# A three-layer graph kernel: 32 row slots in place of 16, indices listed 16 columns at a time, and one semaphore for the four gathers of a group

## What is computed

```
def _rgcn_conv(x, src, dst, edge_type, edge_weight, W, root, bias):
    xj = x[src]
    m = jnp.zeros((xj.shape[0], W.shape[2]), dtype=x.dtype)
    for r in range(W.shape[0]):
        mask = (edge_type == r).astype(x.dtype)[:, None]
        m = m + mask * (xj @ W[r])
    m = m * edge_weight[:, None]
    out = jax.ops.segment_sum(m, dst, num_segments=x.shape[0])
    return out + x @ root + bias
...
msgs = edge_weight[:, None] * x[row]
agg = jax.ops.segment_sum(msgs, col, num_segments=x.shape[0])
return agg @ W.T + b
...
h = jnp.maximum(_layernorm(x, axis=-1), 0.0)
x = x + _L0_gnn_ref(h, edge_index, edge_type_4, edge_weight, ...)
h = jnp.maximum(_layernorm(x, axis=-1), 0.0)
x = x + _L1_gnn_ref(h, edge_index, edge_weight, L1_gnn_W, L1_gnn_b)
```

## Time and profile before

| | |
|---|---|
| Median of 3 runs | 7402.78 us (7398.44 to 7409.87) |
| Span of the profiled execution | 7521.5 us |
| POOL busy | 4442.7 us (59% of the span) |
| PE busy | 3965.3 us (53%), PEld 3719.1 us (49%) |
| DVE busy | 2144.3 us (29%) |
| ACT busy | 502.6 us (7%) |
| Granted clock, mean over the span | 0.623 of full speed |
| DMA | 356.64 MB, 47 GB/s |

### The profile page before, as it was taken

The page is one execution under the profiler, slowest core; times in us unless marked ns, Lnnn a source line. Parts: engine busy times, 40 slices in busy tenths (PEclk is TensorE's granted clock), DMA queues, the critical chain, the costliest instruction groups (busy, mean ns, idle before and its releaser), DMA issues.

```text
span 7521.5 us, 80234 instructions
## 1 busy us (share of the span) xinstructions
PE 3965.3 (53%) x17451; PEld 3719.1 (49%) x17451; DVE 2144.3 (29%) x8672; ACT 502.6 (7%) x1663; POOL 4442.7 (59%) x4701
## 2 busy tenths in 40 slices
PE   3665666555555565665565556663434343343444
PEld 3555555555555555555555555553333333333333
DVE  3332233333332322333323323342222222222222
ACT  3000000000000100000000000021000000000000
POOL 3665666566665565665566556645656666666665
PEclk6666666666666666667677767665555555555555
DMA  4111111111111211111111111112111111111112
GB/s 112 45 45 44 45 45 45 44 45 44 45 44 44 72 45 44 44 45 43 44 44 45 44 44 45 45 52 54 44 42 43 42 43 43 43 43 43 42 43 70
DMA packets 250630, 356.64 MB, mean 47 GB/s; under 512 B 80254, under 2 KB 175586, under 8 KB 250610
## 3 DMA queue, kind: packets, MB, share of 16 engines
q0 software_dynamic: 150048, 307.60, 15.6%
q1 hardware_dynamic: 92262, 44.91, 2.1%
q10 hardware_dynamic: 8300, 3.92, 0.2%
HBM read 330.44 MB, written 25.67 MB: 47 GB/s over the span
## 4 chain that ended last, share of the span: by engine, by line
another core or an unknown queue 45%; PE 24%; issue 17%; DVE 6%; DVEq 6%; ACT 1%; ACTq 1%; DMA 0%; POOL 0%; SPq 0%; POOLq 0%
PE bank L547 13%; PE bank L527 10%; DVE window L756 3%; DVEq L735 3%; DVE acc L739 1%; DVEq L756 1%; DVE idx L748 1%; ACT agg L437 1%; DVEq L748 1%; ACT node L378 0%; PE bank L519 0%; PE bank L515 0%; DVEq L739 0%; PE bank L587 0%
## 5 line engine op out<-in xcount | busy, mean ns | idle before, releaser
L312 POOL DMA_INDIRECT rows<-table,idx x4689 | 4430.2, 945 | 3004.4 <-DVE idx L748 1506.2
L547 PE MATMUL bank<-window,rows 128*128 128x192 f32 (+1 forms) x9378 | 2595.9, 442 | 1138.0 <-DVE window L756 711.1
L547 PEld LDWEIGHTS bank<-window,rows 128*128 128x128 f32 x9378 | 2245.0, 292 | 1258.9 <-issue 655.2
L739 DVE TENSOR_TENSOR acc<-acc,bank 128x48 f32 x1173 | 240.1, 205 | 4920.9 <-remote 3406.8
L756 DVE TENSOR_SCALAR window<-iota,key_col,sw 128x192 f32<-128x192 f32 x3126 | 1001.4, 383 | 0.4 <-DVE key_col L693 0.2
L527 PEld LDWEIGHTS bank<-agg,W2s 128*128 128x128 f32 x3128 | 612.8, 281 | 744.7 <-issue 429.3
L527 PE MATMUL bank<-agg,W2s 128*128 128x48 f32 x3128 | 597.6, 354 | 699.5 <-ACT agg L437 433.7
L527 PEld LDWEIGHTS bank<-agg,W1s 128*128 128x128 f32 x3128 | 603.3, 278 | 701.0 <-ACT agg L437 416.4
L527 PE MATMUL bank<-agg,W1s 128*128 128x48 f32 x3128 | 591.6, 351 | 650.6 <-ACT agg L437 398.5
L527 PE MATMUL bank<-agg,W3T 128*128 128x48 f32 x782 | 248.4, 418 | 994.3 <-ACT agg L437 970.5
L437 ACT ACTIVATE agg<-bank 128x192 f32<-128x192 f32 (+1 forms) x1173 | 330.0, 289 | 6220.5 <-remote 4202.1
(11 more groups left out here) (66 smaller groups left out, 592.1 us busy)
## 6 DMA issues: line engine op xcount, KB each, us to landing
rows<-table,idx POOLq DMA_INDIRECT x4689
table<-node SPq DMA_DIRECT2D x48, 256.0 KB
table<-node SPq DMA_DIRECT2D x7, 896.0 KB
tile_rows<-table SPq DMA_DIRECT2D x98, 64.0 KB
tile_rows<-in_x_dram SPq DMA_DIRECT2D x97, 64.0 KB
out_dram<-node SPq DMA_DIRECT2D x24, 256.0 KB
node<-in_x_dram SPq DMA_DIRECT2D x6, 896.0 KB, 11.4
node<-in_x_dram SPq DMA_DIRECT2D x1, 832.0 KB
```

The costliest lines, as they stand in the source:

```text
L312: eng.indirect_dma_start(out=rows[:, slot, :], out_offset=None, in_=table[r][:, :], in_offset=bass.IndirectOffsetOnAxis(ap=idx[:, slot:slo ...
L547: ins = eng.matmul(agg_ps[q % 2][:, 0:width], rows[:, slot, :], window[:, q % 2, k, 0:width], start=(k == 0), stop=(k == n - 1))
L739: eng.tensor_tensor(a, a, mix_ps[q % 2][:, 0:W], ALU.add).then_inc(s_acc, 1)
```

## The change

The loop iteration becomes eight groups (`GI = 8`, two halves of `HALF = 4`), and so there are 32 row slots, and 49 iterations to a layer in place of 98. `idx`, `rows` and `sw` double. The staging tile for the ends of the layers, and the sum of the general path, which doesn't run on these inputs, lie now inside `rows`. DVE lists the indices and weights of four groups at once: at `q == 1` those of the second half of the same iteration, at `q == 5` those of the first half of the next. POOL waits for a list once in four groups. The four gathers of a group signal one semaphore, for which PE waits once, ahead of the group's first matmul. In the diff the first `fast(r)` is that of POOL; the piece with `s_agg_sb` is PE's, and those with `list_half` are DVE's.

```
-GI = 4
+GI = 8
 NSLOT = CG * GI
+HALF = GI // 2
...
+    OWN = GI // HALF
...
-        stage = sb("stage", [P, BS, TB * P])
...
+        stage = rows[:, 0:BS * TB, :].rearrange("p (s t) d -> p s (t d)", s=BS)
+        gagg = rows[:, BS * TB:BS * TB + R, :].rearrange("p t d -> p (t d)")
...
-        s_row = [sem(f"s_row{k}") for k in range(NSLOT)]
+        s_row = [sem(f"s_row{q}") for q in range(GI)]
...
             def fast(r):
                 def group(i, g, q, n):
-                    eng.wait_ge(s_idx, g + (r * NG + 1))
-                    hold(eng)
+                    if q % HALF == 0:
+
+                        eng.wait_ge(s_idx, i * OWN + (r * NT + q // HALF + 1))
+                        hold(eng)
                     for k in range(q * CG, q * CG + n):
-                        gather(r, k, s_row[k])
+                        gather(r, k, s_row[q])
...
                     if not first(g, 2):
                         eng.wait_ge(s_agg_sb, g + (r * NG - 1))
+                    eng.wait_ge(s_row[q], i * (16 * CG) + (row_base(r, q) + 16 * n))
                     for k in range(n):
                         slot = q * CG + k
-                        eng.wait_ge(s_row[slot], i * 16 + (row_base(r, slot) + 16))
                         ins = eng.matmul(agg_ps[q % 2][:, 0:width], rows[:, slot, :], window[:, q % 2, k, 0:width],
                                          start=(k == 0), stop=(k == n - 1))
...
+                def list_half(i, h):
+
+                    m = HALF * CG
+                    if isinstance(i, int):
+                        m = min(m, C - (i * NSLOT + h * m))
+                    k = h * HALF * CG
+                    c = i * NSLOT + k
+                    eng.tensor_copy(idx[:, k:k + m], src_col[:, bass.ds(c, m)]).then_inc(s_idx, 1)
                     if r < 2:
-                        scale_weights(q * CG, q * CG, CG)
+                        eng.tensor_scalar(sw[:, k:k + m], w_col[:, bass.ds(c, m)], extg[:, 3:4], wscale[:, 0:1],
+                                          ALU.add, ALU.mult).then_inc(s_sw, 1)
+                for h in range(OWN):
+                    list_half(0, h)
...
                         eng.wait_ge(s_agg, g + (T - 1))
-                        if not (isinstance(g, int) and g + 2 >= NG):
-                            m = min(CG, C - (g + 2) * CG) if isinstance(g, int) else CG
-                            k = ((q + 2) % GI) * CG
-                            eng.tensor_copy(idx[:, k:k + m], src_col[:, bass.ds(g * CG + 2 * CG, m)]).then_inc(s_idx, 1)
-                            if r < 2:
-                                scale_weights(g * CG + 2 * CG, k, m)
-                    if r < 2:
-                        eng.wait_ge(s_sw, g + (T + 1))
+                    if q == 1 and not first(i, 1):
+                        list_half(i, 1)
+                    if q == HALF + 1 and not (isinstance(i, int) and i == NI - 1):
+                        list_half(i + 1, 0)
+                    if q % HALF == 0 and r < 2:
+                        eng.wait_ge(s_sw, i * OWN + (r * NT + q // HALF + 1))
```

More of the change, by code:

```diff
@@ L59, in build @@
     split_last = last_rows < P
-    assert D == P and NI == NT and NG - (NI - 1) * GI >= 3 and NG <= 512
+    assert D == P and NI * OWN == NT and NG - (NI - 1) * GI >= HALF + 3 and NG <= 512 and NI > 2
     assert R * P <= 512 and 4 * CT * P + C <= ACC and NB > BS
@@ L110, in build @@
         gwindow = window[:, :, :, :].rearrange("p a c w -> p (a c w)")[:, 0:R * P]
-        gagg = stage[:, 0, :]
+        stage = rows[:, 0:BS * TB, :].rearrange("p (s t) d -> p s (t d)", s=BS)
+        gagg = rows[:, BS * TB:BS * TB + R, :].rearrange("p t d -> p (t d)")
         gtmp = sb("gtmp", [P, 8])
@@ L235, in build, with row_base @@
         stored_all = stored[2] + 16 * (NB - 1 + moves(last_batch))
-        def row_base(r, slot):
-            return 16 * r * (NI - 1 + (slot < last_chunks))
+        def row_base(r, q):
+            return 16 * r * ((NI - 1) * CG + min(CG, max(0, last_chunks - q * CG)))
         block = ctx.enter_context(nc.Block())
@@ L432, in group @@
                 def group(i, g, q, n):
-                    if q == 0 and r < 2:
-                        own(r, i)
+                    if q % HALF == 0 and r < 2:
+                        own(r, i * OWN + q // HALF)
                     eng.wait_ge(s_agg, g + (r * NG + 1))
@@ L551, in group @@
                         mix_group(g - 1, q - 1 + GI)
[L552 to L555, removed]
+                    if q % HALF == 0 and r == 0:
+                        own_turn(i * OWN + q // HALF)
+                    if q % HALF == 1 and r < 2:
+                        own_root(r, i * OWN + q // HALF)
                 over_groups(eng, group)
@@ L760, in group @@
                         add_window(g - 2, q)
-                    if q == 2:
+                    if q % HALF == 2:
                         eng.wait_ge(s_acc, g + (T - 1))
-                        own(r, i)
-                        eng.wait_ge(s_own, i + (r * NT + 1))
+                        own(r, i * OWN + q // HALF)
+                        eng.wait_ge(s_own, i * OWN + (r * NT + q // HALF + 1))
                 eng.wait_ge(s_zero, min(r + 1, 2))
```

6 lines of the change are left out of this document (removed).

## The result

The changed kernel takes **7753.94 us** (median of 4 runs, 7744.41 to 7761.5); the kernel before 7406.32 (4 runs, 7398.44 to 7415.0: the three of the table above, and a fourth of 7415.0). The ratio is **1.047, 95% interval 1.045 to 1.048**: slower, as forecast, and 176 us under the forecast 7930.

The account below looks back on a forecast made before the run. It took PE's results, held back while gathers stream, to set the pace. (782 x 6.9) + (391 x 6.2) + 240.9 = 8061 us of span, times 0.984 gave 7930 us, 7.1% slower; range 6850 to 8650.

Parts of the forecast that it names:

- The hold: PE's results wait while POOL's gathers stream and come out together 3.68 to 5.50 us after the last gather's start.
- Later copies: DVE lists after every fourth addition while POOL stands: 6.53 to 7.5 us a group in layers one and two, 7.0 halfway.
- The third layer's 6.2: Four additions already follow a release there, so the index copy can come right at it: 6.2 us a group.
- The factor 0.984: Runs' median over profiled span (7402.78 / 7521.5), used to turn 8061 us of span into 7930 us.
- Fewer copies: On DVE, 1161 index copies become 98 a layer; 0.1 us a group taken as saved, ends 0 and 0.29.
- one semaphore: PE can't start on a group's first chunk before its fourth lands; 11 us in all, 0.15%, at layer starts.
- longer loop: Half as many loop turns and fewer waits on POOL lie under the hold; shared staging costs nothing.
- The shared port: DVE's copies cost POOL's gathers next to nothing; by the skill, fewer copies would free some 170 us at most.
- Rival 1: The hold goes and POOL runs through at 1.25 us a gather: 6010 us; chance 0.10.
- Rival 2: Gather runs join into 32, as DVE lists while POOL still gathers: 5.77 us a group, 6900 us; chance 0.22.
- Rival 3: PE's own work makes its true ends late; pace stays 6.2 us a group, time near 7400; chance 0.06.

Follow-up runs that it names:

- e1_sem: The kernel before with only one edit: the four gathers of a group signal one semaphore, for which PE waits once; 6091.6 us, ratio 0.9992.
- e5_after: The changed kernel, unedited, measured again beside the kernel before on the second chip; 6088.98 us, ratio 0.999.
- e7_fine2: The changed kernel with lists of four columns at each group, two groups ahead, on the second chip; 6089.32 us, ratio 0.9988.
- e6_before: The kernel before, unedited, measured once more on the second chip; 6097.81 us.

## Why the prediction was right, and where it was off

**The hold**, "PE's results are held back while gathers stream, and come out together some us after the last one": right as a reading of that trace. The bursts, the runs and the gaps are there after the change, and 4.00 us pass from last gather to release where the earlier trace rows had 3.68 to 5.50 (that 5.50 ends at an ACT copy, the others at an addition). It was wrong to think that it belongs to any execution of this kernel: on two of the three chips used later it was absent, and there the change gains 0.1%. That the changed kernel met the hold when it was first measured was luck, for nothing in the prediction says when it comes; the sign of the forecast hung on it.

**Later copies**: the mechanism is right, and its best case is what happened. I worked out 26.1 us for the cycle of the first layer and took 7.0 us a group, half way to the worst pattern with two additions between release and list. That pattern did not come: four additions fell to a cycle, two of them under the gathers as in the earlier trace rows, and the cycle was 26.3 (26.0 and 26.2 on average in the first two layers). **The step that was mis-sized is this term**: 6.9 us a group on the books, 6.48 measured, 782 x 0.42 = 328 us too much. The third layer's 6.2 was 6.22, but only in part by its own reasons: single runs took 6.11 a group, and joined ones, which the term left out, 6.34.

**The factor 0.984** between profiled span and median went the other way. It was no relation of span and time: in every run on record the time lies some 2 us above the span of the same execution (7761.5 and 7759.7 for the profiled one here). The profiled execution of the kernel before was a slower one, with 7521.5 outside its timed runs of 7398.44 to 7415.0 and near the 7511 of the third chip. So 125 us that I took off should have stayed. Against the sum of 8061 us of span: -328 for the first term, +9 for the third layer, +18 outside the stretches gives 7760. With the factor the two errors cancel in part, which is luck: -301 + 125 = -176 us.

**Fewer copies**, **one semaphore** and **longer loop**: small, as said. Where no hold covers them e1_sem, e5_after and e7_fine2 each lie 4 to 8 us below the kernel before, 0.1%; for e1_sem the interval includes no difference. The 0.1 us a group taken for the fewer copies under the hold was tested by no run. The +18 us outside the stretches were not in the sum. None lies before the first gather, which starts at 94.9 us in both traces. Some 3 come from the earlier trace rows, whose stretches end about 1 us later than those here; the other 15 lie behind the last gather of each layer (42.1 us to the next layer's first for 36.8, 77.3 for 74.9, 44.7 to the end for 37.3). Without the hold, in e5_after and e6_before, the same three differ by 0.5, 1.9 and 1.3 us, and not in one direction. What makes them longer under the hold wasn't looked into.

**The shared port**: e7_fine2 and e5_after differ by 879 index copies and take 6089.32 and 6088.98 us. The loss that I worked out by the Trainium skill, SBUF - State Buffer, part on DVE blocking DMA, does not show here; a gather takes 946 ns in both.

**Rival 1**, the hold goes: its picture and its time came true (6010 stated, though 6102 x 0.984 is 6004; 6089 measured), for both kernels and for another reason than the change. **Rival 2**, runs join: it was right that they can, and 26 runs in the third layer did. Its price was wrong. The joined run shown takes 51.1 us from 6106.82 to 6157.87, 6.38 a group and not 5.77, because behind the release, 5 us after the last gather, three more additions had to pass before the list, where my price had none. So joining gave nothing: the 19 runs of 32 average 6.34 a group, the 44 of sixteen 6.11. **Rival 3**, PE is the bound: fallen. In e6_before PE has more busy time (4684.3 us against 3965.3) and the whole takes 1425 us less (spans of 6096.0 and 7521.5). The Trainium skill, Perfetto Trace Analysis, section on the per-instruction lifecycle, says that PE's end is an estimate; that stays so, but it wasn't what made the additions late.

**What stays open** is what holds the results, and why in some measurements only. Each group of runs was on one chip and at one time, and no chip was used twice, so the hold can belong to the chip as well as to the time; running both kernels again on one of the chips would tell, and wasn't done. The traces give a hint. The records of semaphore updates by DMAs number 17731 and 16785 in the two first traces with the hold, and 79771 and 79804 in e6_before and e5_after, for the same 4689 gathers; on the third chip they number 18094 to 29132. They go missing as the hold sets in: from the first gather of the third layer on, the kernel before has 43, 23, 9, 7 and 6 of them in steps of 5 us, and e6_before 46, 66, 63, 65 and 64, while POOL issues four or five gathers a step in both. A hold and missing records go together in all thirteen traces with gathers. The Trainium skill, NOTIFIC — the notification-queue block, section on overflow, says that a full queue of records, by its setting, loses records or stalls who writes them. Here records are missing and results are late in the same traces. No run shows a stall of that kind, and every timed execution was a recorded one, so it is not more than a hint. It wasn't tried to bring the hold on by more recorded traffic.

## What to carry to other kernels

When several engines wait for an unnamed releaser and are let go together after another engine's burst, ask first whether that wait is there in a second measurement, on another chip too: here it was worth 1310 to 1415 us and decided the sign of the change. Under such a hold a feeder stops until its consumer gets to the next list, so count the steps from release to list; with the stall made by hand a larger batch cost nothing where its list was the first thing behind the release (third layer), and one step of 2 us for each sixteen gathers where it was not. Without the hold, 1.25 us a gather on POOL sets the time, and listing, lead and number of semaphores are worth 0.1%.

## What the runs showed of the hardware

**The clock differs with how PE's waits are cut.** By stretch, the first layer of e6_before and of e5_after (the last column but two is the granted clock, as a share of full speed):

```profile
95.28:2053.84 1958.56, 1711.01 (x6519) 1405.85 (x6519) 750.46 (x2814) 150.09 (x489) 1482.65 (x1563) 0.62 0.22 56
```

```profile
95.06:2049.52 1954.46, 1401.77 (x6515) 1343.36 (x6516) 652.22 (x2232) 149.77 (x488) 1478.49 (x1562) 0.74 0.22 56
```

With a semaphore for each slot PE's matmuls wait for rows 2567 times over the span and PE is granted 0.62 of full speed in this layer on average, nearer to the lower level (1.2 GHz, 0.50) than to the upper (2.4 GHz). With one for four gathers they wait for rows 1089 times and PE is granted 0.74; its busy time in this layer falls by 309 us. The rest of the change stands in that pair too, but e1_sem, which has the semaphore alone, has a mean of 0.668 over the span against 0.588, and its PE busy time is 3783.0 us against 4684.3 (e6_before, on the second chip). POOL was the bound, and so none of this came out in the time. The third layer, of the same two kernels, says that the busy time isn't the clock's alone: both are granted 0.50, and it falls all the same, from 1190.0 to 914.8 us (4113.15 to 6064.17 in e6_before, 4102.74 to 6052.91 in e5_after).
